# GpSimd's sums placed apart in time from VectorE's one-hots and low halves

## What is computed

```
x = layernorm(x + Wu([x, gat2(gat1(layernorm(x)))]))          # first layer
mean[r, n] = mean of x[src] over edges of relation r into n    # 34 relations
h1 = sum_r mean[r] @ W_rel[r] + x @ W_root + b_rgcn
xw = h1 @ W_gcn
out = segment_sum(xw[src] * dinv[src] * dinv[dst], dst) + xw * dinv * dinv + b_gcn
x = layernorm(x + out)
```

## Time and profile before

| what | value |
| --- | --- |
| median of 3 runs | 3539.23 us (3531.12 to 3541.21) |
| the profiled execution | 3537.14 us |
| its span | 3535.4 us |
| granted TensorE clock, mean | 0.966 of full speed |
| busy: TensorE, VectorE, ScalarE, GpSimd | 3221.4, 2313.1, 1452.9, 1733.3 us |
| GpSimd's sums of weights, L679, L685, L687, L693 | 35 each, 2636, 2794, 2791, 2646 ns mean |
| one-hots L1621 | 360, 517 ns mean |
| low halves of x L1557 | 35, 971 ns mean |

### The profile page before, as it was taken

One profiled execution on the slowest core, in us unless ns is written; L12 is line 12 of the kernel. 1 busy time (PEld: TensorE's weight loads), 2 busy tenths in 40 slices (PEclk: granted clock), 3 DMA queues, 4 the chain that ended last, 5 costly groups with the idle time before them and its releaser, 6 DMA issues. The chain is left out here.

```text
span 3535.4 us, 59936 instructions
## 1 busy us (share of the span) xinstructions
PE 3221.4 (91%) x17157; PEld 1992.4 (56%) x17157; DVE 2313.1 (65%) x4671; ACT 1452.9 (41%) x2650; POOL 1733.3 (49%) x1418
## 2 busy tenths in 40 slices
PE   6989988975669999999999999999999998979998
PEld 3444456875435555555555666666666664535545
DVE  8999995758844544544556787887888854533324
ACT  2767735645333443333334554545555442100100
POOL 2710037873234443443414565665656614777771
PEclk9999999997779999999999999999999999989999
DMA  3010022010233323333334555554545534675551
GB/s 94 2 45 0 0 62 96 1 28 8 84 98 120 134 101 127 128 109 120 123 122 140 166 189 159 183 169 163 190 159 189 163 134 138 174 233 157 157 132 52
DMA packets 228601, 411.06 MB, mean 116 GB/s; under 512 B 36596, under 2 KB 179443, under 8 KB 228518
## 3 DMA queue, kind: packets, MB, share of 16 engines
q1 hardware_dynamic: 166272, 266.73, 21.8%
q0 software_dynamic: 60000, 141.97, 14.9%
q10 hardware_dynamic: 2246, 1.29, 0.1%
HBM read 260.86 MB, written 148.95 MB: 116 GB/s over the span
## 5 line engine op out<-in xcount | busy, mean ns | idle before, releaser
L2112 PE MATMUL bank<-arena 128*128 128x384 f16 x3675 | 1202.8, 327 | 23.1 <-ACT arena L1109 13.3
L2114 PE MATMUL bank<-arena 128*128 128x384 f16 x3675 | 1201.4, 327 | 0.0
L2115 PE MATMUL bank<-arena 128*128 128x384 f16 x3675 | 1201.1, 327 | 0.0
L1109 ACT ACTIVATE arena<-bank,winv 128x384 f32<-128x384 f32 x700 | 398.4, 579 | 989.7 <-PE bank L2115 973.4
L1657 DVE SCALAR_TENSOR_TENSOR arena<-bank,winv,arena 128x384 f32<-128x384 f32 x525 | 317.4, 614 | 427.6 <-PE bank L2115 426.4
L2112 PEld LDWEIGHTS bank<-arena 128*128 128x128 f16 x3675 | 360.4, 98 | 283.2 <-ACT arena L1109 24.4
L2115 PEld LDWEIGHTS bank<-arena 128*128 128x128 f16 x3675 | 360.5, 98 | 239.3 <-issue 2.9
L2114 PEld LDWEIGHTS bank<-arena 128*128 128x128 f16 x3675 | 360.8, 98 | 233.1 <-issue 7.6
L740 POOL DMA_INDIRECT arena<-y_half,idx_now x360 | 404.1, 1122 | 120.5 <-issue 92.9
L1550 DVE SCALAR_TENSOR_TENSOR arena<-arena,wscale 128x1152 f16<-128x1152 f32 x245 | 367.7, 1536 | 141.3 <-ACT arena L1032 133.1
L668 POOL DMA_INDIRECT typ_s<-rel_inv_dram,idx_w x240 | 271.3, 1130 | 328.9 <-DMA rel_inv_dram<-src_s 255.5
(11 more groups left out here) (244 smaller groups left out, 4284.3 us busy)
## 6 DMA issues: line engine op xcount, KB each, us to landing
y_half<-arena SPq DMA_DIRECT2D x306, 384.0 KB
arena<-in_L_gnn_W_rel_dram SPq DMA_DIRECT2D x68, 1152.0 KB, 8.2
arena<-y_half,idx_now POOLq DMA_INDIRECT x720, 3.2
y_half<-arena SPq DMA_DIRECT2D x34, 294.0 KB
cT_dram<-arena SPq DMA_DIRECT2D x1, 5625.0 KB
arena<-cT_dram SPq DMA_DIRECT2D x9, 625.0 KB
arena<-in_x_dram SPq DMA_DIRECT2D x10, 384.0 KB, 9.5
typ_s<-rel_inv_dram,idx_w POOLq DMA_INDIRECT x240, 2.7
```

What stands on the lines that cost most here:

```text
L1109: nc.scalar.activation(y[half][:, :, c * CQ:(c + 1) * CQ], acc, ACT.Copy, scale=scale).then_inc(r_copied, 1)
L2112: nc.tensor.matmul(acc, h, w_hi[m - 1][:, k, :], start=fresh and k == 0, stop=False, skip_group_check=True)
L2114: nc.tensor.matmul(acc, h, w_lo[m - 1][:, k, :], start=False, stop=False, skip_group_check=True)
L2115: ins = nc.tensor.matmul(acc, l, w_hi[m - 1][:, k, :], start=False, stop=k == KH - 1, skip_group_check=True)
```

## The change

Three edits, all of order or waiting; no instruction of work is added or removed.

- x1_sums(m), GpSimd: before its four sums it also waits until VectorE has written the three low halves of the same pair's blocks (x1_lo at least 7m + 3).
- rows_step, GpSimd (the 15 edge steps): t1_t2 for the next weights stands behind the gathers of units 4 and 5, where it stood ahead of them, right behind t3.
- one_step, VectorE: measure(.., 1) stands right behind measure(.., 0), ahead of edge_low of unit 3, where it stood behind it. Without edges both orders are the same.

```diff
@@ x1_sums, GpSimd
                 a, b, s = x1T[2 * m % 4], x1T[(2 * m + 1) % 4], xsum[m % 2]
                 pool.wait_ge(x1_turned, 2 * m + 2)
+                pool.wait_ge(x1_lo, 7 * m + 3)
                 if m >= 2:
@@ rows_step, GpSimd
                 gather(q - 1, i, PER, 3)
                 t3(next_q, next_i)
-                t1_t2(next_q, next_i)
                 gather(q - 1, i, PER, 4)
                 gather(q - 1, i, PER, 5)
+                t1_t2(next_q, next_i)
@@ one_step, VectorE
                     edge_add(q - 1, i, PER, 1)
                 measure(next_q, next_i, 0)
+                measure(next_q, next_i, 1)
                 if edges:
                     edge_low(q - 1, i, PER, 3)
-                measure(next_q, next_i, 1)
                 if edges:
                     edge_add(q - 1, i, PER, 2)
```

## The result

The changed kernel takes 3522.24 us (median, 3518.31 to 3526.74), the kernel before, run beside it, 3535.57: the ratio is 0.9962, with a 95% interval of 0.9949 to 0.9975, so 13.3 us less (9 to 18). The forecast was 3545 and 3528 to 3560. It missed, and by its sign too. Of the 23 us between 3545 and 3522.24 some 4 are the kernel before itself, whose median of six runs is 3535.57 where the three that the forecast started from gave 3539.23.

A forecast was written before the change was run, and what follows sets the result against it. TensorE's gaps were taken to bound the edge steps, VectorE's row x1. Steps +14 less x1's 7.5 gave +6.5: 3543.6 from the profiled 3537.1, 3545.7 against the median, written as 3545, range 3528 to 3560.

The forecast's parts named there:

- The bound, and the hold: Steps gain only from TensorE's gaps, x1 from its last low half; VectorE instructions started beside a GpSimd sum outlast it.
- x1, a pair: x1, blocks 0 to 3: 4.98 us becomes 2.01, less 0.9 for holds, saving 2.07 x 4 = 8.3 us.
- the short chain: x1, next tile's rsqrt chain beside the fourth sum: held, 0.9 us taken off each pair, bounds nothing to 0.99.
- x1, the last block: End of x1: no next tile hides the sums, so the last low ends 990.8 against 989.95, 0.8 us lost.
- Unit 3's gap goes wholly: Edge steps, fourth unit: one-hots no longer meet sums, so TensorE's gap goes, 19.1 us over 15 steps.
- Unit 4's gap: Edge steps, fifth unit: t1_t2's sums hold its one-hots; gap 2.15 us where the old was 1.34, 12 us lost net.
- with 12.95 instead of 13.2 it is 8: Edge steps: t1_t2 starting 12.95 us after t3, not 13.2, makes the net loss 8 us instead of 12.
- The clock: Edge steps: longer one-piece gaps cause one more drop of TensorE's clock, 2 us, bounds 0 and 4 drops (7 us).
- rival called slower: Unit 4's gap long enough to drop the clock in four or five more steps: +18, 3557; chance 0.15.
- the rival called even: Gathers 0.5 us shorter, nothing behind the maximum in TensorE's queue: steps 0, x1 -9, 3530; chance 0.15.
- the 0.6 and the 13.2: Unit 4: 0.6 us from VectorE's maximum to TensorE's load; t1_t2 starts 13.2 us after t3.
- Gathers held by one-hots: Edge steps, unit 4's gathers: the skill's rule would slow them all; set aside because the last gather took 1.15 us.

The follow-up runs named there:

- t1_t2 alone: Kernel before with only t1_t2 moved behind the gathers of units 4 and 5: 3541.97 us, ratio 1.0012 (second group); 3947.92, ratio 0.9905, on the slower chip.
- the changed kernel's second profile: The changed kernel run again, unaltered, in the second group: 3525.91 us, ratio 0.997 against the kernel before.
- the orders alone: Kernel before with t1_t2 behind the gathers and both measure calls first, no wait in x1: 3533.93 us, ratio 0.9993; on the slower chip 3963.3, 0.995.
- w_scaled here: 20 us: Changed kernel with t1_t2 also waiting for VectorE's next weights' scale: 3507.18 us, ratio 0.9915 against the kernel before; edge steps 20.0 us less than the changed kernel.
- one and the same edit: Only t1_t2 moved behind the gathers, against the kernel before: 3541.97 us, ratio 1.0012, in the second group; 3947.92, ratio 0.9905, on the slower chip.

## Why the prediction was wrong

**The bound, and the hold.** Right. TensorE's gaps are what the steps can give, the last low half is what ends x1, and the credit's 16.33 us came through unchanged. A one-hot or a low half that starts beside a sum does not end before the sum: every row above that is held shows it.

**x1, a pair.** Right in mechanism; what it saves was put 1.7 us too low. 2.97 us saved ahead of the add, as forecast (4.98 to 2.00 is 2.98). For the short chain 0.9 was taken off, and 0.65 - 0.16 = 0.49 was lost: only L1423 was held, and the sum that held it had already run 0.36 us. Four pairs give 2.49 x 4 = 10.0 instead of 8.3. The Trainium skill (SBUF — State Buffer, section Who interferes with whom) has two SBUF inputs as what makes an instruction wait for GpSimd's reads. The trace agrees: L1423 was held to the sum's end (927.90 against 927.89), and not so the next tile's adds (one of two inputs from PSUM, 0.51 each) and its statistics (0.56 and 0.54), which have one. How much a short chain loses depends on where its instructions start: L1421 started at 926.86, 0.03 us ahead of the fourth sum, and slipped through, L1420 at 926.66 had 0.15 of a sum left and took 0.17, and only L1423 met most of one.

**x1, the last block.** Right: 0.8 lost was forecast, 0.9 measured. x1 in sum 9.5 (the terms give 9.1), where 7.5 with bounds 5 and 11 was forecast.

**Unit 3's gap goes wholly.** Right: 19.1 us of 19.1.

**Unit 4's gap.** The place and the mechanism were right, the size was not, and this is the step that failed: 2.1 us a step was forecast, 1.2 came (18.0 over 15), and the sign hung on the difference. Two terms:

- From L1527's end to TensorE's first product 0.6 us was put, because the register instructions in TensorE's queue ran until 0.4 after it. It is 0.13. Those instructions run beside the first product and hold nothing up: in the earlier trace rows there were 1.6 us of slack between the last of them and the product, so the rows showed when they ran and not that anything waited for them. 0.47 x 15 = 7 us.
- L1527 itself ends 0.4 us earlier after t3 than forecast: in the mean 12.96 after the point at which unit 3's products start, where the forecast's terms give 13.4. t1_t2 starts 12.9 us after t3, not 13.2. That is 0.3 x 15 = 4.5 us. The forecast read the span of the eight gathers of before wrongly: it took the first of them, 1.30 us, as one with nothing of VectorE beside it, and so the 1.15 of the last as plain. The rows of before, VectorE beside the first gather (2121.84) and beside the last two (2129.70 and 2131.32):

```profile
2121.70 0.61 DVE L1623 SCALAR_TENSOR_TENSOR agg_lo<-arena,typ_s,agg_hi 128x384 fp32r<-128x384 f32 x1
...
2129.59 0.61 DVE L1623 SCALAR_TENSOR_TENSOR agg_lo<-arena,typ_s,agg_hi 128x384 fp32r<-128x384 f32 x1
...
2131.04 0.61 DVE L1623 SCALAR_TENSOR_TENSOR agg_lo<-arena,typ_s,agg_hi 128x384 fp32r<-128x384 f32 x1
```

Each of the three gathers starts while a low half runs, 0.14, 0.11 and 0.28 us after the low half's start, and takes 1.30, 1.32 and 1.15; the five others take 0.94 or 0.95. Those three are 0.9 us of the 10.63, and behind t3 most of it is not there (the first gather took 0.96 in the step shown). Some 1.5 us more of the 6 is that the weights landed slightly earlier, and perhaps that in eight steps only one one-hot was held; this part was not taken apart. In the prediction's own terms this was the step "with 12.95 instead of 13.2 it is 8".

**The clock.** One more drop was forecast, 2 us; none came. With 2.52 in one piece the largest gap is where the largest was. That the length of the gap decides, as the forecast and its rival called slower had it, does not hold in the other traces: with t1_t2 alone the waits of 2.27 and 2.54 us ahead of unit 4's products are followed by a drop (0.64 and 0.73 in the next 4 us) and the longest, 2.69 us, between them, is not; in the changed kernel's second profile one of 2.16 is and one of 2.67 is not.

The sum of the steps: 14 - 7 - 6 - 2 = -1, measured -0.5 (-2.3 by the medians of the orders alone, 932.0 to 942.1 being the spread of such stretches). The outcome is nearly the rival called even (steps 0, x1 -9, 3530), which had 0.15 and named both reasons: gathers half a microsecond shorter, and nothing behind the maximum in TensorE's queue. The -13.3 of the medians is 4 us beyond it, inside the measurement's interval. The range should have reached further down: the bounds of the steps were +8 to +23, though two of the terms, the 0.6 and the 13.2, each had zero or the lower value in sight, worth 7 and 4 us. They were bounded one at a time, and the sum took neither end.

**Gathers held by one-hots.** The Trainium skill's other rule (SBUF — State Buffer, the box on VectorE blocking DMAs of the GpSimd queue) says that descriptors are not written while VectorE runs a double-port instruction. It was right to set it aside for the one-hots: in the step shown a gather with a one-hot beside it took 0.95 us, as plain ones do. The reason given was wrong, since the rows of before do show a hold, by the low halves: in the changed kernel, too, the gather at 2424.53, 0.09 us behind the start of a low half, took 1.34.

## What to carry to other kernels

Moving an instruction that holds another engine back moves the hold to whatever stands there, so place it by a wait on the work it must miss (w_scaled here: 20 us) and not by its position in a queue, whose time depends on when a DMA lands. Where the sign of a forecast hangs on a difference of two nearly equal gaps, bound every latency in it from zero. And look at the largest gap of the stretch first: the one at unit 0, which this change left alone, was worth more than the two that it traded, and in the step that was read it also delayed the loads for the next step.

## What was not expected of the hardware

- The hold goes both ways. A sum of GpSimd that starts while a low half of VectorE runs (L687 at 2119.05 in the step shown, behind the low half of 2118.99) takes 3.01 to 3.03 us in all 15 steps of the changed kernel. It is the low half that costs this 0.4 us and not the held one-hot: the sums that held a one-hot without a low half at their start took 2.63 to 2.64 (7 of them in the changed kernel).
- Register instructions in TensorE's queue behind a wait do not delay the product that waited: 0.13 us from the end of VectorE's maximum to the first product, with four such instructions between 2124.4 and 2124.7 in the step shown.
- The same program took 3536 to 3537 us on two chips and 3986 on a third, and one and the same edit was worth +4 on one of the first two and -38 on the third.
